# A macaron transformer block on one core: fewer waits on TensorE, products on zeroed memory at the start, and a turned copy of the values written by ScalarE

## The reference, cut to what matters

```
x = x + 0.5 * channel_mix(layernorm(x))
x = x + t5_attention(layernorm(x))          # 16 heads of 64, full 512x512 scores
x = x + 0.5 * channel_mix(layernorm(x))
x = x + 0.5 * local_layers(layernorm(x))    # 2 layers, 8 heads, window of 64
x = x + gru(layernorm(x))                   # a scan over the tokens
x = x + 0.5 * local_layers(layernorm(x))
```

```
q, k, v = h @ wq, h @ wk, h @ wv            # per head [512, 64]
scores  = q @ k.T + bias(relative position)
out     = softmax(scores) @ v
return out @ wo
```

## Time and profile before

| | |
|---|---|
| median of three runs | 1226.47 us |
| the profiled execution, its time | 1225.16 us |
| its span, first to last instruction | 1223.1 us |
| TensorE busy, matmuls | 1141.3 us (93%) |
| VectorE busy | 908.0 us (74%) |
| ScalarE busy | 885.9 us (72%) |
| GpSimd busy | 607.6 us (50%) |
| granted TensorE clock, mean | 0.990 of full speed |

### The profile page before, as it was taken

How to read it: one execution, slowest core, us unless ns; L and a number is a source line. 1 busy time by engine, 2 the same in 40 slices (tenths; PEclk the granted TensorE clock), 3 DMA queues, 4 the chain that set the end, 5 groups by cost and what they waited for, 6 DMA issues and landing times.

```text
span 1223.1 us, 39937 instructions
## 1 busy us (share of the span) xinstructions
PE 1141.3 (93%) x15750; PEld 694.1 (57%) x15750; DVE 908.0 (74%) x2425; ACT 885.9 (72%) x2390; POOL 607.6 (50%) x396
## 2 busy tenths in 40 slices
PE   4889999999999988799999999989999899999997
PEld 1355655555555553366666666655556566666664
DVE  2498888888988875687777777767677777777773
ACT  4676666666666557688877978866878778877874
POOL 0266565665656552466554654442535346554640
PEclk9999999999999999899999999999999999999999
DMA  4622222222322222411111210110111102111110
GB/s 156 250 62 74 62 71 64 61 74 55 81 55 76 58 55 69 109 32 32 40 31 28 49 38 21 32 31 18 31 27 40 32 19 49 40 33 26 40 40 18
DMA packets 35481, 66.71 MB, mean 55 GB/s; under 512 B 6704, under 2 KB 8176, under 8 KB 35296
## 3 DMA queue, kind: packets, MB, share of 16 engines
q1 hardware_dynamic: 35296, 64.16, 19.9%
HBM read 15.32 MB, written 1.11 MB: 13 GB/s over the span
## 4 chain that ended last, share of the span: by engine, by line
PE 79%; issue 6%; ACT 5%; DVE 4%; DMA 2%; SPq 2%; POOL 2%; DVEq 0%; ACTq 0%; POOLq 0%
PE ps L483 11%; PE ps L462 9%; PE ps L1407 6%; PE ps L1370 5%; PE ps L1337 5%; PE ps L1307 5%; PE ps L1286 4%; PE ps L1276 4%; PE ps L1349 4%; PE ps L1377 4%; PE ps L1277 3%; PE ps L491 2%; PE ps L1413 2%; PE ps L448 2%; PE ps L431 2%
## 5 line engine op out<-in xcount | busy, mean ns | idle before, releaser
L415 POOL TENSOR_TENSOR arena<-arena 128x1024 f32<-128x1024 f32 x128 | 241.2, 1895 | 173.4 <-DVE arena L657 173.4
L568 ACT ACTIVATE arena<-arena 128x512 f32<-128x512 f32 x256 | 182.5, 714 | 134.5 <-DVE arena L643 134.4
L1231 POOL TENSOR_TENSOR arena<-arena 128x1024 f32<-128x1024 f32 x64 | 121.5, 1898 | 227.3 <-DVE arena L1786 227.3
L1611 ACT ACTIVATE arena<-arena 128x128 f32<-128x128 f32 x512 | 198.2, 390 | 30.7 <-DVE arena L1778 30.1
L643 DVE CUSTOM_DVE_ANT_0 arena<-ps,arena 128x512 f32<-128x512 f32 x256 | 164.4, 688 | 44.4 <-PE ps L462 41.8
L1778 DVE CUSTOM_DVE_ANT_0 arena<-ps,near,arena 128x128 f32<-128x128 f32 x512 | 144.5, 346 | 40.2 <-PE ps L1337 40.1
L483 PEld LDWEIGHTS ps<-arena 32*64 32x64 f32 x8192 | 122.4, 132 | 70.5 <-issue 43.9
L653 DVE STREAM_TRANSPOSE arena<-arena 128x1024 f32<-128x1024 f32 x128 | 156.7, 1232 | 2.3 <-POOL arena L415 2.0
L483 PE MATMUL ps<-arena 32*64 32x128 f32 x8192 | 140.2, 277 | 17.1 <-issue 13.1
L1238 POOL TENSOR_TENSOR arena<-arena 128x1024 f32<-128x1024 f32 x64 | 151.1, 2362 | 0.0
L462 PE MATMUL ps<-arena 64*128 64x512 f32 x512 | 141.1, 632 | 3.0 <-issue 1.2
(11 more groups left out here) (176 smaller groups left out, 2103.5 us busy)
## 6 DMA issues: line engine op xcount, KB each, us to landing
arena<-arena SPq DMA_DIRECT2D x191, 128.0 KB, 2.4
arena<-arena SPq DMA_DIRECT2D x64, 192.0 KB, 2.6
arena<-rel_rows SPq DMA_DIRECT2D x16, 448.0 KB, 9.0
arena<-arena SPq DMA_DIRECT2D x64, 64.0 KB, 2.1
arena<-y SPq DMA_DIRECT2D x30, 128.0 KB, 2.3
arena<-arena SPq DMA_DIRECT2D x15, 127.8 KB, 2.4
arena<-in_wqkv SPq DMA_DIRECT2D x2, 768.0 KB, 5.3
x<-in_x SPq DMA_DIRECT2D x4, 256.0 KB, 5.2
```

The lines of the kernel that those rows point to most:

```text
L415: nc.gpsimd.tensor_tensor(e, e, scale, ALU.mult).then_inc(self.normed, 1)
L568: nc.scalar.activation(self.e[:, r % 3, i, :], self.neg[:, i, :], ACT.Exp, bias=self.nmax[:, i:i + 1], scale=-1.0, accum_out=self.sums[:, ...
L1611: nc.scalar.activation(self.e[:, s, h, :], self.neg[:, h, :], ACT.Exp, bias=self.nmax[:, h:h + 1], scale=-1.0, accum_out=self.sums[:, s, h ...
```

## The change

It does four things.

- TensorE's waits for `ot_made` ahead of the three projections, and those for `q_read` and `k_read` ahead of the second round of scores, are left out. In TensorE's order an earlier instruction has already waited for the same or more.
- TensorE first waits for the two clears of y only, and then runs 18 products of 128x128 by 128x320 on the zeroed plane of y into bank 7, which nobody reads before it is written anew. Then it waits for the loads. Its wait for all eleven steps of `prepared` is gone.
- `copy_v` becomes three instructions on ScalarE: the copy of 128x512, and two of 64x512 that write the copy turned by 64 partitions. The semaphore `v_read` is raised by the last of the three.
- SyncE makes only the copies turned by 32 and 96: four DMAs per unit instead of six, and the counts of `v_spread` follow.

```diff
+WARM = 18
...
-                sp.wait_ge(self.v_spread, 96 * u)
+                sp.wait_ge(self.v_spread, 64 * u)
...
-            for j in range(1, self.GROUPS):
+            for j in range(1, self.GROUPS, 2):
...
         def q_proj(u):
...
-            if u >= 3:
-                pe.wait_ge(self.ot_made, u - 2)
...
         def k_proj(u):
...
-            if u >= 3:
-                pe.wait_ge(self.ot_made, u - 2)
...
         def v_proj(u):
...
-            if u >= 3:
-                pe.wait_ge(self.ot_made, u - 2)
...
         def score(r, pair):
...
-            if pair == 0:
+            if pair == 0 and r % 2 == 0:
                 pe.wait_ge(self.q_read, u + 1)
                 pe.wait_ge(self.k_read, u + 1)
...
-                pe.wait_ge(self.v_spread, 96 * (u + 1))
+                pe.wait_ge(self.v_spread, 64 * (u + 1))
...
         def copy_v(u):
...
-                act.wait_ge(self.v_spread, 96 * (u - 2))
-            nc.scalar.activation(self.v[:, u % 3, 0, :, :].rearrange("p a b -> p (a b)"), V, ACT.Copy).then_inc(self.v_read, 1)
+                act.wait_ge(self.v_spread, 64 * (u - 2))
+            v = self.v[:, u % 3, :, :, :].rearrange("p j t c -> p j (t c)")
+            nc.scalar.activation(v[:, 0, :], V, ACT.Copy)
+            nc.scalar.activation(v[0:P // 2, 2, :], V[P // 2:P, :], ACT.Copy)
+            nc.scalar.activation(v[P // 2:P, 2, :], V[0:P // 2, :], ACT.Copy).then_inc(self.v_read, 1)
...
             @block.tensor
             def _(pe):
+                pe.wait_ge(prepared, 2)
+                for _ in range(WARM):
+                    nc.tensor.matmul(k.ps[:, 7, 0:320], k.y[:, B, 1:1 + P], k.y[:, B, 1:1 + 320], start=True, stop=True)
                 pe.wait_ge(k.loaded, 48)
-                pe.wait_ge(prepared, 11)
```

## The result

The changed kernel takes **1257.22 us** (median of four runs, 1254.18 to 1259.13) against 1226.59 for the kernel before (also of four runs, the three named above and one of 1228.90): a ratio of **1.023**, 95% interval [1.021, 1.026]. The forecast said slower, and 1234.0; the range ended at 1244. The profiled execution took 1256.54 us, its span is 1254.7. A measured 31.6 us of span were lost where 7.5 were forecast.

What follows compares the result with a forecast made beforehand. TensorE, busy throughout undisturbed attention turns, was taken as the bound. 1225.16 + 17.3 (V copy) - 8.8 (gaps) - 1.0 (start) = 1232.7 us for the profiled execution, 1234.0 us as median; range 1222 to 1244.

Steps and rivals of the forecast that it cites:

- the V copy: ScalarE's three-part copy frees V's bank late, so TensorE idles ahead of turns: 0.57 us per turn, 17.3 us lost.
- the gaps: TensorE's issue gaps at borders of fetched pieces: seven bad turns and one clock fall, 13.7 against 22.5 us, 8.8 gained.
- the start: Products on zeros ahead of TensorE's first real work raise its clock earlier: a gain of 1 us.
- the restart: TensorE starts the next turn 0.04 us after the third V copy ends, as ScalarE does behind TensorE.
- The upper bound: V copy's worst case: 0.60 us per added copy and no overlap, 0.81 us per turn, 24 us in all.
- The term for the first turn: First weighing turn waits for the V copy until 75.13 us instead of starting at 74.40: 0.77 us lost.
- rival 2: TensorE's fetch gaps stay, or the clock falls in most of the seven turns: 1243 us; chance 0.17.
- The waits left out: TensorE's redundant waits: directly nothing, but fewer instructions move the fetch borders, part of the 8.8 us gain.
- The products on zeros: TensorE's first real matmul at 13.8 us, ScalarE's first inversion at 16.6 instead of 17.50: a gain of 1 us.
- Rival 1: Fewer DMAs free TensorE's instruction fetches and remove all gaps: 1220 us; chance 0.15 in both its forms.
- its second form: ScalarE's added V copies cost only 0.26 us each, 4 us in all: 1221 us; shares the chance of 0.15.
- Rival 3: V's copy isn't late at the turn's start, because v_read isn't last: 1217 us; chance 0.02.

Runs made afterwards that it cites:

- e7: Changed kernel with four kinds of turned V copy by unit modulo 4, only for reading durations (doesn't compute the block); ran once, 1244.69 us.
- e6: Changed kernel with one line moved, so that weigh names v_read first of its six waits: 1239.57 us, 1.012 of the kernel before.
- e3: Kernel before with only the redundant waits left out: 1220.32 us, 0.994 of the kernel before.
- e1: Changed kernel with the V copy and SyncE's six DMAs put back as before: 1220.18 us, 0.995 of the kernel before.
- e4: Kernel before with only the 18 products on zeros and TensorE's shorter first wait: 1224.61 us, 0.999 of the kernel before.
- e2: Kernel before with only the three-part V copy and SyncE's four DMAs per unit: 1261.97 us, 1.029 of the kernel before.
- e9: e1 with weigh's waits put where they are needed, none alone at the head of a turn: 1208.50 us, 0.986 of the kernel before.
- e12: Kernel before with only weigh's waits put where they are needed, as in e9: 1207.74 us, 0.982 of the kernel before.
- e11: e1 with v_read named first of weigh's waits, the line moved in e6: 1225.12 us, 0.998 of the kernel before.
- e8: e1 with 26 products of 222 columns in place of 18 of 320: 1215.83 us, 0.991 of the kernel before.

## Why the prediction was wrong, point by point

**Direction and place were right, the size was not.** The forecast had 17.3 us for the V copy, less 8.8 for the gaps, less 1.0 for the start: +7.5 us. Measured in the spans: +33.4 for the turns, -0.8 for gaps and clock, -0.9 for start and end. The way of the move was forecast for the right reason; the copy's term, which decides, came out at half its size, and the gain from the gaps hardly came.

**The copy of V: the term that failed.** The mechanism is as put: TensorE idle ahead of every turn, ScalarE the releaser, the exponentials not much later, SyncE's saving worth nothing. The term was 0.57 us a turn, and 1.15 were measured. Two pieces were mis-sized. The third copy's end: 0.48 us were taken from start to start "as same columns and source are nearest", and it is 0.61, since a copy that reads from another start partition doesn't overlap the one before (e7): 2 x 0.13 = 0.26 us. And the restart: 0.04 us were taken from ScalarE's start behind TensorE, where nothing stands between the semaphore and the copy. On TensorE that is right for the first wait-only instruction, but three stand in front of the weight load, 0.11 us each; with v_read carried by the weight load the 0.36 us fell to 0.05 (e6): 0.31 us. Together 0.57, within 0.01 us what was missing. The upper bound that I had set, 0.81 us a turn, took the copies at 0.60 but left the restart at 0.04: so a cost that was carried over from another engine was given no bound. The term for the first turn, 0.77 us, didn't show as such: there the third copy ended at 73.85 and TensorE started at 74.06.

**The gaps.** The places were right: units 2, 6, 10 to 26, with 12 products to go, and none elsewhere. e3, e1, e4 and e2 had theirs in the units that were named too. The price was too low. One gap turn was put at 1.71 us, from the turn of unit 3, one of the two cheapest: the others of the kernel before without a fall of the clock lost up to 2.05. And one fall was put at 1.7: 13.7 us in all. Measured 20.2: the four turns without a fall cost 1.8 to 2.5 us each (the gap itself is 1.69, not 1.41, in the one shown), and three, not one, were followed by a fall. The part of rival 2 by which more gaps are followed by a fall came in, but not for its reason: e1 has no wait for the V copy ahead of its gaps, and in its profiled execution four of seven were followed by one. How often the clock falls differs from run to run of one kernel (e1: 1215 to 1227 us). One reading was off as well: the ninth gap inside `weigh`, 1.6 us in unit 29, lies behind the 29 turns and so isn't part of the 20.9 us; the sum that adds it apart is right.

**The waits left out.** "Directly nothing" fits, and of the 8.8 us through the instruction stream 5.6 were found where the copy isn't in the way (e3, against the kernel before beside it).

**The products on zeros.** The first inversion came at 16.13 us against 16.6 forecast, and TensorE's real work began at 13.26 against 13.8. The clock rose sooner than forecast: 8 of the 36 instructions ran at the half clock and 28 at the full one, not 10.4 and 25.6. The gain was 1.4 us there, and the attention's first projection came 2.0 us earlier, but of that 0.3 reached the first weighing turn. The clock fell again in between, at 67 us, behind gaps of 0.78 and 1.11 us in the scores of the first units, where the kernel before had no fall (columns as in the earlier trace rows):

```profile
66.00:71.00 5.00, 5.00 (x9) 1.81 (x9) 5.00 (x14) 4.12 (x12) 4.30 (x3) 0.66 0.15 45
```

That is 1.7 us, as much as was missing. e4 shows no gain in the whole, but its interval, [0.996, 1.001], has room for one of 1 us.

**Rival 1** (the fetches are freed by fewer DMAs) is refuted by e2, and its second form by the added copies, which last 0.59 us and not 0.26. What does free them is where the waits stand (e9, e12), which no rival had. **Rival 3** (`v_read` isn't last) is refuted by the 29 waits for the third copy.

**What stays open.** Records show how long a wait-only instruction is held and when packets move, but not when a piece is asked for: that the request waits with the sequencer is inferred from these times and from e6, e9, e11 and e12. Why the packet is on its way so much sooner for the border behind 200 in e8 than for those behind 194 and 198 in the kernel before wasn't settled. Nor do the runs say why some gaps are followed by a fall of the clock and others aren't.

## What to carry to other kernels

When an engine has no slack, ask of every instruction that is put in front of a semaphore who waits for it: 1.2 us of free time on ScalarE cost 33 us because a PSUM bank was held, and cost nothing once the bank was given back first. Where an engine waits for several semaphores, put each wait on the first instruction that needs it and let the one that comes last be carried by a real instruction: without any other change that took 1.8% off this kernel. And price the restart behind a wait from a place with as many waits in front of it.

## What the runs showed of the hardware that wasn't expected

- A copy on ScalarE whose source in PSUM starts at another partition than that of the one before it starts 0.59 to 0.61 us after it; one that starts at the same partition 0.48 to 0.50 us (512 columns, e7). Whether it has 64 partitions or 128 made no difference.
- Wait-only instructions at the head of a dense stretch of TensorE cost 0.11 us each behind the semaphore that comes last, 0.3 us for three (e6), and go with gaps of 1.3 to 2.0 us some 2 us later, in turns whose instruction packet moves only 0.8 to 1.6 us after the start (in the kernel before, the changed one, e1 and e11). With the waits moved the packet comes before the turn, and the gaps are gone (e9) or all but one (e12).
- TensorE's granted clock fell to half behind some of these gaps only: behind 18 of the 73 early ones in ten profiled executions, none of them shorter than 1.60 us, at about 1.7 us lost each.
- The length of an instruction stream ahead of a loop can be worth microseconds: 32 instructions more and nearly as many columns moved the gaps to other turns (e8 against e1). The times differ by 4 us, but the intervals of the two ratios, 0.991 and 0.995, just overlap. The waits left out moved gaps too and took 5.6 us off (e3).
